# Two small activations of the query factors move one step on in ScalarE's order

## The chip, the cores and the metric

The kernel runs on one core of a Trainium2 chip. The metric is the device time of one launch in microseconds; of several runs the median is told. The engines are called PE (TensorE), DVE (VectorE), ACT (ScalarE), POOL (GpSimd) and SP (SyncE, which issues the transfers here). Each of them takes its own instructions strictly in order and waits for the others on semaphores.

## What is computed

The input is 4 sequences of 512 rows of 128 numbers. A first layer (an attention of 16 heads with alibi) is followed by six local layers, and the change lies in these. One local layer does, cut to what matters:

```
q, k, v = split(shift_tokens(x) @ Wqkv)            # 16 heads of 64
q = l2norm(q) * qs;  k = l2norm(k) * ksc           # then both are rotated by tables
sim  = einsum(q, k of this and the last window of 32) * 8.0,  masked
attn = softmax(sim);  x = (attn @ v) @ Wo + x
xn   = layernorm(shift_tokens(x));  a, gate = split(xn @ W1 + b1)
x    = a * gelu(gate) @ W2 + b2 + x
```

The norm of q is not applied to q. It is kept as one factor for each row and head, `rq = 8 / |q|`, and goes in as the scale of the exponential of the scores: `prob = exp(rq * s_in + lower)`, with `lower = -max(s_in) * rq`.

## The kernel before

The local layers are a software pipeline. A *unit* is one layer of one sequence (24 units), a *quarter* is 4 of the 16 heads of a unit (96 quarters), and a loop over 105 steps `s` is written out on each engine. In step `s` the engines work on several quarters at once: `n = s` is projected and normed, `c = s - 1` is scored, the weights of `d = s - 2` are exponentiated, and those of `e = s - 3` are transposed and applied to the rows (`weigh_rows`). The program's own order on each engine, and nothing else, decides what runs first; `after(engine, semaphore, n)` is a wait for the n-th signal.

The order of ACT in a step is: once in four steps (`s` = 11, 15, ... ) the gelu of a unit, between two loads of the function table (L1010, L1015, L1017); 5, 3 and 8 exponentials of `d` (L1001), with the squares of the k projection between them (`sq`, L1026 and L1031); the squares of the q projection (L1037, L1039); the copies `zT` (L997, two); logarithm and exponential of the key factors `rk` (L1048, L1050); those of the query factors `rq` (L1053, L1055); and once in four steps (`s` = 1, 5, 9, ...) the copy `xk_own` (L997) and the normed rows `xnT` (L1064). Two kinds of step are spoken of below: a **gelu step** is one that begins with the gelu, an **xnT step** is one that ends with `xk_own` and `xnT`.

What stands around these on the other engines:

- PE: k projection (L862), output projection `bank_y` (L881), q projection (L862) into the same `bank_a`, which must wait until both squares of k are taken (`sqk_ok`, L1031), `weigh_rows` (L873), the sum over a key head (L946), scores (L894), the sums over the query heads (L956), turns of the rows (L907, in the xnT step), first half of the feed forward (`bank_f` and `bank_z`, L902: the gate's product is the last thing in the step ahead of a gelu step).
- DVE: the rotation products `pk` and `pq` (L1135 to L1142), the transpose `pT` (L1156), the floor of the key sums (L1178), `den` (L1181), the masked scores `s_in` (L1188, L1190), the floor of the query sums `rq_sum` (L1196, signals `floorq_ok`), the row maxima `s_max` (L1200).
- POOL: `sumk` (L1090), `pk` (L1092, L1093), `sumq` (L1096), `qfin` (L1099, L1100), `kfin` (L1104, L1105, needs `rk`), and at the end of the step `lower` of quarter `c` (L1110, needs `rq` of `c` and `s_max`), for which the exponentials of the next step wait.

Of the kernel before, what the change touches and what calls it, by code (L numbers as in the profile page):

```python
# [14 lines left out]
ACT = mybir.ActivationFunctionType  # L15
# [692 lines left out]
def local_layers(nc, args, state, held):  # L708
# [4 lines left out]
    with ExitStack() as ctx:  # L713
        def sb(name, shape, dt=F32):
            return ctx.enter_context(nc.sbuf_tensor(name, shape, dt))
# [4 lines left out]
        def sem(name):  # L720
# [13 lines left out]
        rq = sb("rq", [P, 2, TPB * GH])  # L734
        rq_sum = sb("rq_sum", [P, TPB * GH])
        log8 = sb("log8", [P, 1])
# [33 lines left out]
        sqk_ok, sqq_ok, lnk_ok, rk_ok, lnq_ok, rq_ok, exp_ok, z01_ok, z23_ok, xk_ok, xnT_ok, gelu_ok = map(  # L770
            sem, ["sqk_ok", "sqq_ok", "lnk_ok", "rk_ok", "lnq_ok", "rq_ok", "exp_ok", "z01_ok", "z23_ok", "xk_ok",
                  "xnT_ok", "gelu_ok"])
        sqk0_ok, sqq0_ok, pk2_ok, pq2_ok = map(sem, ["sqk0_ok", "sqq0_ok", "pk2_ok", "pq2_ok"])
        pk_ok, pq_ok, floor_ok, den_ok, rden_ok, pT_ok, mask_ok, max_ok, floorq_ok, lower_ok = map(
            sem, ["pk_ok", "pq_ok", "floor_ok", "den_ok", "rden_ok", "pT_ok", "mask_ok", "max_ok", "floorq_ok", "lower_ok"])
# [5 lines left out]
        def after(eng, s, n, each=1):  # L781

            if n >= 0:
                eng.wait_ge(s, (n + 1) * each)

        def quarter(n):
            return 0 <= n < QUARTERS

        def unit_at(s, stage):

            u, left = divmod(s - LAG_FF - stage, GROUPS)
            return u if left == 0 and 0 <= u < UNITS else None

        def rows_at(s):

            u, left = divmod(s - 1, GROUPS)
            return u if left == 0 and 0 <= u < UNITS else None

        def layer_of(u):
            return u // B  # L800
# [193 lines left out]
        @block.scalar  # L994
        def _(act):
            def copy(out, in_):
                return act.activation(out, in_, ACT.Copy)  # L997

            def exponentials(n, lo, hi):
                for i in range(lo, hi):  # L1000
                    last = act.activation(prob[:, n % 2, i, :], s_in[:, n % 2, i, :], ACT.Exp,  # L1001
                                          bias=lower[:, n % 2, i:i + 1], scale=rq[:, n % 2, i:i + 1])
                return last

            def step(s):
                n, c, d, e = s, s - 1, s - 2, s - 3
                u_back, u_gelu = unit_at(s, 2), unit_at(s, 4)
                u_rows = rows_at(s)
                if u_gelu is not None:
                    act.preload_act_table(ACT.Gelu)  # L1010
                    after(act, gate_mm, u_gelu)
                    after(act, ff_mm, u_gelu - 1)
                    for j, bank in ((2, bank_f), (0, bank_z[:, 2, :]), (1, bank_z[:, 3, :])):
                        m = min(P, FF - j * P)
                        last = act.activation(hid[0:m, j, :], bank[0:m, :], ACT.Gelu, bias=b_gate[0:m, j:j + 1])  # L1015
                    last.then_inc(gelu_ok, 1)
                    act.preload_act_table_set("natural_log_exp_and_others")  # L1017
                if quarter(d):
                    after(act, lower_ok, d)
                    after(act, pT_ok, d - 2)  # L1020
                    after(act, den_ok, d - 2)
                    exponentials(d, 0, 5)
                if quarter(n):
                    after(act, k_mm, n)
                    after(act, sumq_ok, n - 1)
                    act.activation(sq[:, 0, :], bank_a[:, 0, :], ACT.Square).then_inc(sqk0_ok, 1)  # L1026
                if quarter(d):
                    exponentials(d, 5, 8)
                if quarter(n):
                    after(act, pk2_ok, n)  # L1030
                    act.activation(sq[:, 1, :], bank_a[:, 1, :], ACT.Square).then_inc(sqk_ok, 1)  # L1031
                if quarter(d):
                    exponentials(d, 8, TPB * GH).then_inc(exp_ok, 1)
                if quarter(n):
                    after(act, q_mm, n)
                    after(act, sumk_ok, n)
                    act.activation(sq[:, 0, :], bank_a[:, 0, :], ACT.Square).then_inc(sqq0_ok, 1)  # L1037
                    after(act, pq2_ok, n)
                    act.activation(sq[:, 1, :], bank_a[:, 1, :], ACT.Square).then_inc(sqq_ok, 1)  # L1039
                if quarter(e):  # L1040
                    after(act, z_mm, e)
                    after(act, y_mm, e - 2)
                    z = zT[:, e % 2].rearrange("p w t h q -> p w (t h q)")
                    copy(z[:, 0:2, :], bank_z[:, 0:2, :]).then_inc(z01_ok, 1)
                    copy(z[:, 2:4, :], bank_z[:, 2:4, :]).then_inc(z23_ok, 1)
                if quarter(n):
                    after(act, floor_ok, n)
                    act.activation(rk[:], rk[:], ACT.Ln).then_inc(lnk_ok, 1)  # L1048
                    after(act, lnk_ok, n)
                    act.activation(rk[:], rk[:], ACT.Exp, scale=-0.5).then_inc(rk_ok, 1)  # L1050
                    after(act, floorq_ok, n)
                    after(act, lower_ok, n - 2)
                    act.activation(rq[:, n % 2], rq_sum[:], ACT.Ln).then_inc(lnq_ok, 1)  # L1053
                    after(act, lnq_ok, n)
                    act.activation(rq[:, n % 2], rq[:, n % 2], ACT.Exp, bias=log8[:], scale=-0.5).then_inc(rq_ok, 1)  # L1055
                if u_rows is not None:
                    after(act, xk_mm, u_rows)
                    after(act, z_mm, 4 * (u_rows - 2) + 3)
                    copy(xk_own[:, u_rows % 2].rearrange("p t c -> p (t c)"), bank_z[:, 2, :]).then_inc(xk_ok, 1)
                if u_back is not None:  # L1060
                    after(act, ffn_loaded, layer_of(u_back), 16)
                    after(act, xnT_mm, u_back)
                    after(act, lin_mm, u_back - 1)
                    act.activation(xnT[:], bank_z[:, 3, :], ACT.Identity, bias=ln_b, scale=ln_g).then_inc(xnT_ok, 1)  # L1064

            act.preload_act_table_set("natural_log_exp_and_others")
            act.wait_ge(const_ok, 1)
            for s in range(STEPS_ALL):
                step(s)
# [418 lines left out]
```

## Time and profile before

| what | value |
|---|---|
| median of 3 runs | 2041.87 us (2039.39 to 2042.81) |
| the profiled execution, its time | 2042.99 us |
| its span, first to last instruction | 2040.9 us |
| mean granted TensorE clock | 0.968 |
| busy: PE, DVE, ACT, POOL | 90%, 76%, 68%, 62% |

The local layers take the span from about 420 us to 2016 us. From about 580 us on they repeat with one period for each unit (four steps), and a busy share is a mean over steps of different kinds, so the timeline of one period tells more than the shares do.

### The profile page before, as it was taken

The numbers are of one execution on the slowest core, as the hardware profiler recorded it, in microseconds if no ns is written. First come the engines' busy times: TensorE is split into PE (matmuls) and PEld (weight loads), VectorE is DVE, ScalarE is ACT, GpSimd is POOL, SyncE is SP. The second block draws the span as 40 slices with busy tenths as digits, with TensorE's granted clock in tenths as the row PEclk, the third lists the DMA queues.
The fourth block names the chain that finished last, engine by engine and source line by source line (L and its number), as shares of the span: only waits on it lengthen the run. The fifth ranks groups of instructions, "written<-read, shape, count | busy, mean of one in ns | idle before, by whom it ended". The sixth has DMA issues, their size and how long they took to land. (4 is left out here: it accounts for less than half of the span.)

```text
span 2040.9 us, 47434 instructions
## 1 busy us (share of the span) xinstructions
PE 1835.3 (90%) x18048; PEld 1023.9 (50%) x18048; DVE 1544.4 (76%) x2543; ACT 1383.9 (68%) x2862; POOL 1263.2 (62%) x1127
## 2 busy tenths in 40 slices
PE   5898898668999999999999999999999999999984
PEld 3443344524555555555555555555555555555541
DVE  4778886257877788788887888878887788877753
ACT  1454445237777777877778777778777877778851
POOL 4303300057877777777777787777877778777721
PEclk8899999769999999999999999999999999999996
DMA  9000000215323343233432234332343322233300
GB/s 192 2 2 1 2 2 2 63 46 98 75 69 75 81 89 75 68 71 82 87 80 69 68 81 86 74 79 68 75 88 74 83 68 69 67 77 84 71 22 21
DMA packets 142992, 131.86 MB, mean 65 GB/s; under 512 B 85160, under 2 KB 88808, under 8 KB 142440
## 3 DMA queue, kind: packets, MB, share of 16 engines
q1 hardware_dynamic: 142768, 128.83, 28.4%
q8 instruction: 145, 2.38, 0.5%
q14 instruction: 79, 0.65, 0.1%
HBM read 20.94 MB, written 1.05 MB: 11 GB/s over the span
## 5 line engine op out<-in xcount | busy, mean ns | idle before, releaser
L1001 ACT ACTIVATE prob<-s_in,lower,rq 128x64 f32<-128x64 f32 x1536 | 537.9, 430 | 79.0 <-POOL lower L1110 77.0
L862 PE MATMUL bank_a<-x_shift,wqk_sb 128*128 128x512 f32 x768 | 375.2, 612 | 69.1 <-ACT sq L1031 57.5
L881 PE MATMUL bank_y<-zT,wvo 128*128 128x512 f32 x768 | 345.2, 592 | 0.0
L1090 POOL TENSOR_TENSOR sumk<-sq 128x512 f32<-128x512 f32 x96 | 122.3, 1274 | 271.6 <-ACT sq L1031 271.6
L862 PEld LDWEIGHTS bank_a<-x_shift,wqk_sb 128*128 128x128 f32 x768 | 140.1, 193 | 262.0 <-issue 148.4
L881 PEld LDWEIGHTS bank_y<-zT,wvo 128*128 128x128 f32 x768 | 146.0, 190 | 183.7 <-issue 183.7
L894 PEld LDWEIGHTS bank_z<-kpad,qpair 128*32 128x32 f32 x6144 | 164.6, 110 | 100.1 <-issue 98.8
L894 PE MATMUL bank_z<-kpad,qpair 128*32 128x128 f32 x6144 | 187.7, 274 | 23.2 <-ACT zT L997 23.2
L491 DVE TENSOR_REDUCE a_negmax<-a_max 128x1 f32<-128x512 f32 x256 | 164.7, 685 | 47.9 <-PE a_max L166 44.3
L382 ACT ACTIVATE a_prob<-a_sT 128x1024 f32<-128x1024 f32 x128 | 130.5, 1023 | 103.7 <-PE a_sT L216 101.8
L997 ACT ACTIVATE zT<-bank_z 128x1024 f32<-128x1024 f32 x192 | 186.1, 1023 | 10.7 <-PE bank_z L873 8.0
L1078 POOL TENSOR_TENSOR prob<-prob,rden 128x1024 f32<-128x1024 f32 x96 | 182.9, 1905 | 3.9 <-DVE rden L1184 3.9
L1096 POOL TENSOR_TENSOR sumq<-sq 128x512 f32<-128x512 f32 x96 | 122.0, 1270 | 92.5 <-ACT sq L1039 92.5
L873 PE MATMUL bank_z<-pT,xk_prev 32*128 32x128 f32 x3072 | 164.8, 284 | 3.2 <-DVE xn L1162 1.7
L873 PEld LDWEIGHTS bank_z<-pT,xk_prev 32*128 32x128 f32 x3072 | 122.4, 187 | 78.4 <-issue 56.1
L873 PE MATMUL bank_z<-pT,xk_own 32*128 32x128 f32 x3072 | 154.8, 271 | 0.0
L1135 DVE SCALAR_TENSOR_TENSOR pk<-bank_a,scale_sb,rot_sb 128x512 f32<-128x512 f32 x96 | 71.8, 748 | 104.3 <-PE bank_a L862 94.3
L461 POOL TENSOR_TENSOR a_rstd<-a_mv,eps 128x4 f32<-128x4 f32 x4 | 0.8, 198 | 232.8 <-DVE a_mv L549 232.8
L1099 POOL TENSOR_TENSOR qfin<-pq 128x512 f32<-128x512 f32 x96 | 123.7, 1289 | 0.0
L873 PEld LDWEIGHTS bank_z<-pT,xk_own 32*128 32x128 f32 x3072 | 123.0, 188 | 0.0
L1141 DVE SCALAR_TENSOR_TENSOR pk<-bank_a,scale_sb,rot_sb 128x512 f32<-128x512 f32 x96 | 71.6, 746 | 67.6 <-ACT sq L1026 67.6
L1104 POOL TENSOR_TENSOR kfin<-rk,pk 128x512 f32<-128x512 f32 x96 | 122.1, 1272 | 0.5 <-ACT rk L1050 0.5
(161 smaller groups left out, 3947.3 us busy)
## 6 DMA issues: line engine op xcount, KB each, us to landing
qpair<-qfin SPq DMA_DIRECT2D x384, 128.0 KB, 2.3
kpad<-kfin SPq DMA_DIRECT2D x768, 64.0 KB, 2.0
wqk_sb<-in_wqkv SPq DMA_DIRECT2D x24, 256.0 KB, 5.6
xk_prev<-xk_own SPq DMA_DIRECT2D x24, 192.0 KB, 2.4
ffn_sb<-in_ffn SPq DMA_DIRECT2D x6, 537.5 KB, 3.9
wv_in<-in_wqkv SPq DMA_DIRECT2D x12, 256.0 KB, 4.8
wo_in<-in_wo SPq DMA_DIRECT2D x6, 512.0 KB, 5.8
xk_prev<-xk_own SPq DMA_DIRECT2D x24, 48.0 KB, 2.1
```

Of the source, the lines that this page charges most:

```text
L382: act.activation(prob[:, j % 2, 2 * half:2 * half + 2, :], sT_bank[:, 2 * half:2 * half + 2, :], ACT.Exp).then_inc(exp_ok, 1)
L491: dve.tensor_reduce(negmax[:, unit // 4, unit % 4:unit % 4 + 1], max_bank[u % 2][:], AX.X, ALU.max, negate=True).then_inc(max_ok, 1)
L862: last = pe.matmul(bank_a[:, half, :], wqk_sb[:, layer_of(u) % 2, part, half, g * P:(g + 1) * P], cols(u), start=True, stop=True)
L873: last = pe.matmul(bank_z[:, w, t * P:(t + 1) * P], rows[at, u % 2, t, :], pT[at, n % 2, c, t * GH:(t + 1) * GH, :].rearrange("p h q -> p ...
L881: last = pe.matmul(bank_y[:].rearrange("p (t w q) -> p t w q", w=WPT, q=WIN), wvo[:, layer_of(u), GH * g + hh, :], zT[:, n % 2, :, :, hh, ...
L894: last = pe.matmul(bank_z[WIN * w:WIN * w + WIN, t // 2, c:c + P], qpair[:, p, at:at + WIN], kpad[:, p, :, at:at + 2 * WIN], start=True, s ...
L997: return act.activation(out, in_, ACT.Copy)
L1001: last = act.activation(prob[:, n % 2, i, :], s_in[:, n % 2, i, :], ACT.Exp, bias=lower[:, n % 2, i:i + 1], scale=rq[:, n % 2, i:i + 1])
L1078: pool.tensor_tensor(prob[:, e % 2], prob[:, e % 2], rden[:].unsqueeze(2).broadcast_to([P, TPB * GH, 2 * WIN]), ALU.mult).then_inc(pn_ok, 1)
L1090: pool.tensor_tensor(sumk[:], sq[:, 0, :], sq[:, 1, :], ALU.add).then_inc(sumk_ok, 1)
L1099: pool.tensor_tensor(qfin[:, 0, :], pq[:, 0, :], pq[:, 1, :], ALU.subtract)
L1104: pool.tensor_tensor(kfin[:, 0, :], rk[:], pk[:, 0, :], ALU.mult)
```

## The change

The two activations of `rq` leave the end of step `n`, and stand in step `n + 1` (where that quarter is `c`), behind the gelu and its second table load and ahead of the exponentials of `d`. Their two waits move with them. Nothing is added, removed or resized on any engine.

```diff
@@ act step(s) @@
                     last.then_inc(gelu_ok, 1)
                     act.preload_act_table_set("natural_log_exp_and_others")
+                if quarter(c):
+                    after(act, floorq_ok, c)
+                    after(act, lower_ok, c - 2)
+                    act.activation(rq[:, c % 2], rq_sum[:], ACT.Ln).then_inc(lnq_ok, 1)
+                    after(act, lnq_ok, c)
+                    act.activation(rq[:, c % 2], rq[:, c % 2], ACT.Exp, bias=log8[:], scale=-0.5).then_inc(rq_ok, 1)
                 if quarter(d):
                     after(act, lower_ok, d)
                     after(act, pT_ok, d - 2)
...
                     after(act, lnk_ok, n)
                     act.activation(rk[:], rk[:], ACT.Exp, scale=-0.5).then_inc(rk_ok, 1)
-                    after(act, floorq_ok, n)
-                    after(act, lower_ok, n - 2)
-                    act.activation(rq[:, n % 2], rq_sum[:], ACT.Ln).then_inc(lnq_ok, 1)
-                    after(act, lnq_ok, n)
-                    act.activation(rq[:, n % 2], rq[:, n % 2], ACT.Exp, bias=log8[:], scale=-0.5).then_inc(rq_ok, 1)
```

In a step that ends without `xk_own` and is followed by one without gelu nothing stood between the two places, so ACT's order is the same there. It differs at two places.

The first is ACT at the border from step 10 to step 11, the first gelu step. Before, the pair of `rq` stands ahead of the table load:

```order
L1048 ACTIVATE rk<-rk 128x512
L1050 ACTIVATE rk<-rk 128x512
L1053 ACTIVATE rq<-rq_sum 128x16
L1055 ACTIVATE rq<-rq,log 128x16
L1010 ACT_TABLE_LOAD
L1015 ACTIVATE hid<-bank_f,ffn_sb 85x512
L1015 ACTIVATE hid<-bank_z,ffn_sb 128x512 x2
L1017 ACT_TABLE_LOAD
L1001 ACTIVATE prob<-s_in,lower,rq 128x64 x5
```

Now it stands between the second load and the exponentials (the lines of the changed file are six further on behind the added lines):

```order
L1054 ACTIVATE rk<-rk 128x512
L1056 ACTIVATE rk<-rk 128x512
L1010 ACT_TABLE_LOAD
L1015 ACTIVATE hid<-bank_f,ffn_sb 85x512
L1015 ACTIVATE hid<-bank_z,ffn_sb 128x512 x2
L1017 ACT_TABLE_LOAD
L1021 ACTIVATE rq<-rq_sum 128x16
L1023 ACTIVATE rq<-rq,log 128x16
L1001 ACTIVATE prob<-s_in,lower,rq 128x64 x5
```

The pair moved past two table loads and three gelus.

The second is ACT at the border from step 9 to step 10, the end of an xnT step. Before:

```order
L1050 ACTIVATE rk<-rk 128x512
L1053 ACTIVATE rq<-rq_sum 128x16
L1055 ACTIVATE rq<-rq,log 128x16
L997 ACTIVATE xk_own<-bank_z 128x512
L1064 ACTIVATE xnT<-bank_z,ffn_sb 128x512
L1001 ACTIVATE prob<-s_in,lower,rq 128x64 x5
```

And now:

```order
L1056 ACTIVATE rk<-rk 128x512
L997 ACTIVATE xk_own<-bank_z 128x512
L1065 ACTIVATE xnT<-bank_z,ffn_sb 128x512
L1021 ACTIVATE rq<-rq_sum 128x16
L1023 ACTIVATE rq<-rq,log 128x16
L1001 ACTIVATE prob<-s_in,lower,rq 128x64 x5
```

Here it moved past one copy and one activation. PE, DVE, POOL and SP keep their instructions and their order.

## Rows read from the trace of the kernel before

**Rows 1.** The page: busy time by engine, and the slices.
```profile
PE 1835.3 (90%) x18048; PEld 1023.9 (50%) x18048; DVE 1544.4 (76%) x2543; ACT 1383.9 (68%) x2862; POOL 1263.2 (62%) x1127
...
PE   5898898668999999999999999999999999999984
...
PEclk8899999769999999999999999999999999999996
```

**Rows 2.** Windows, from one unit's first gelu to the next one's.
```profile
580.18:644.44 64.26, 61.35 (x647) 35.23 (x646) 52.22 (x83) 50.20 (x111) 49.09 (x43) 1.00 0.31 71
1030.00:1094.24 64.24, 61.34 (x647) 35.23 (x646) 52.23 (x83) 50.19 (x111) 49.06 (x43) 1.00 0.33 80
1865.38:1929.63 64.25, 61.35 (x647) 35.23 (x646) 52.22 (x83) 50.21 (x111) 49.05 (x43) 1.00 0.30 71
```

**Rows 3.** Waits between 580 and 1945 us: total, times, longest.
```profile
POOL sumk L1090 <- ACT sq L1031: 244.6, 85, 5.4
...
ACT rq L1053 <- DVE rq_sum L1196: 123.2, 84, 1.5
...
ACT prob L1001 <- POOL lower L1110: 59.3, 42, 1.5
...
PE bank_a L862 <- ACT sq L1031: 41.1, 22, 1.9
```

**Rows 4.** Timeline of ACT around one gelu step.
```profile
1025.66 0.63 ACT L1050 ACTIVATE rk<-rk 128x512 f32<-128x512 f32 x1
1027.75 0.22 ACT L1053 ACTIVATE rq<-rq_sum 128x16 f32<-128x16 f32 x1 [1.47 <-DVE rq_sum L1196]
1028.00 0.31 ACT L1055 ACTIVATE rq<-rq,log 128x16 f32<-128x16 f32 x1
1028.33 1.28 ACT L1010 ACT_TABLE_LOAD   x1
1030.00 0.68 ACT L1015 ACTIVATE hid<-bank_f,ffn_sb 85x512 f32<-85x512 f32 x1 [0.39 <-PE bank_f L902]
1030.58 1.25 ACT L1015 ACTIVATE hid<-bank_z,ffn_sb 128x512 f32<-128x512 f32 x2
1031.85 1.28 ACT L1017 ACT_TABLE_LOAD   x1
1033.14 1.76 ACT L1001 ACTIVATE prob<-s_in,lower,rq 128x64 f32<-128x64 f32 x5
...
1036.28 0.58 ACT L1031 ACTIVATE sq<-bank_a 128x512 f32<-128x512 f32 x1
```

**Rows 5.** Timeline of PE in the same stretch.
```profile
1027.14 1.96 PE L902 MATMUL bank_z<-xnT,ffn_sb 128*128 128x512 f32 x4
1028.94 1.02 PE L902 MATMUL bank_f<-xnT,ffn_sb 128*85 128x512 f32 x2
1029.80 1.88 PE L862 MATMUL bank_a<-x_shift,wqk_sb 128*128 128x512 f32 x4
1031.51 3.60 PE L881 MATMUL bank_y<-zT,wvo 128*128 128x512 f32 x8
1036.98 1.95 PE L862 MATMUL bank_a<-x_shift,wqk_sb 128*128 128x512 f32 x4 [1.87 <-ACT sq L1031]
```

**Rows 6.** DVE and POOL in the same stretch.
```profile
1035.42 0.75 DVE L1141 SCALAR_TENSOR_TENSOR pk<-bank_a,scale_sb,rot_sb 128x512 f32<-128x512 f32 x1 [2.30 <-ACT sq L1026]
...
1036.93 1.28 POOL L1090 TENSOR_TENSOR sumk<-sq 128x512 f32<-128x512 f32 x1 [5.44 <-ACT sq L1031]
```

**Rows 7.** Timeline of all engines at the end of one xnT step.
```profile
1013.78 0.31 ACT L1055 ACTIVATE rq<-rq,log 128x16 f32<-128x16 f32 x1
...
1013.99 0.58 ACT L997 ACTIVATE xk_own<-bank_z 128x512 f32<-128x512 f32 x1
...
1014.47 0.77 ACT L1064 ACTIVATE xnT<-bank_z,ffn_sb 128x512 f32<-128x512 f32 x1
...
1015.05 0.23 POOL L1110 TENSOR_TENSOR lower<-s_max,rq 128x16 f32<-128x16 f32 x1
...
1015.32 1.10 ACT L1001 ACTIVATE prob<-s_in,lower,rq 128x64 f32<-128x64 f32 x3
```

**Rows 8.** PE there, its q projection in the next step too.
```profile
1012.91 0.64 PE L907 MATMUL bank_z<-ident,x_shift 128*128 128x128 f32 x4
1013.39 0.60 PE L907 MATMUL bank_z<-ident,xn 128*128 128x128 f32 x4
...
1019.15 1.96 PE L862 MATMUL bank_a<-x_shift,wqk_sb 128*128 128x512 f32 x4
```

## The prediction

> **What bounds the kernel now.** I read the page first, then the waits, then one period engine by engine. The page says that PE is busy for 90% of the span and ACT for 68%, with the clock near full in the local layers [rows 1]. That alone would say that ACT has room and that two activations of 16 columns may stand anywhere. The windows from gelu to gelu show how regular the pipeline is: each unit takes 64.25 us, at a granted clock of 1.00 (the higher level, 2.4 GHz), and PE is busy for 61.35 us of it [rows 2]. So PE is idle for 2.90 us in a period, and the question is only where these are and who makes them. The waits between 580 and 1945 us answer it: PE waits for `sq` L1031 22 times, 41.1 us in all, which is 1.87 us each [rows 3]. There are 22 gelu steps in which exponentials follow (steps 11, 15, ... 95), so this is one stall in each gelu step, and PE idles for hardly more than a microsecond elsewhere in the period (2.90 - 1.87 = 1.03 us).
>
> The reader is to see the gelu step in the timelines. ACT loads the gelu's table at 1028.33, has it at 1029.61, waits 0.39 us for the gate's product, starts the gelus at 1030.00, loads the other table at 1031.85 and starts the exponentials at 1033.14 with no gap; the square of k that frees `bank_a` starts at 1036.28 and ends at 1036.86 [rows 4]. PE is through with `bank_y` at 1035.11, and its q projection starts at 1036.98, 0.12 us after the square's end, with the 1.87 us of idleness ahead of it [rows 5]. DVE waits in the same step for the square ahead of it (2.30 us), and POOL for L1031 (5.44 us) [rows 6]. So in a gelu step all three other engines wait for ACT, and ACT itself runs without a gap from 1030.00 to that square. ACT, which is idle for a third of the time, is the bound of this stretch.
>
> **The change part by part.** Nothing is removed or added; one pair moves, with its semaphores. No transfer is issued by it, and no queue but ACT's is touched.
>
> *Where the order stays.* In two of four steps the pair keeps its place between `rk` and the exponentials: no cost and no gain. The wait for `rq_sum` (1.47 us) and the one for `lower` that follows it go on as they are there.
>
> *Gelu step, what it gains.* The pair today waits 1.47 us for DVE's `rq_sum`, and ends at 1028.31. Without it ACT can load the gelu's table as soon as `rk` is done, at 1026.29, that is 2.04 us earlier [rows 4]. That is worth nothing: the gelus wait for the gate's product, whose last matmul ends at 1028.94 + 1.02 = 1029.96 [rows 5], and the gelu starts 0.04 us later. That matmul stands behind four others that run without a gap, so PE's own order sets it. The table load then ends at about 1027.58, and ACT waits 2.43 us in place of 0.39.
>
> *Gelu step, what it costs.* The pair now stands behind the second table load, in the stretch where ACT has no gap. From the start of the logarithm to that of the exponential are 0.25 us, and from there to the next activation 0.21 us where the next one waits for nothing (1013.78 to 1013.99) [rows 4, 7]; its inputs are long there, since `rq_sum` is done before 1027.75. So the exponentials start at 1033.14 + 0.46 = 1033.60 (`lower` came at about 1029.6 and isn't waited for). The bounds: without any overlap it is 0.22 + 0.03 + 0.31 = 0.56 us; below 0.46 I see nothing, since the second activation needs the first one's result. Before, these 0.46 us were covered by ACT's wait for the gate; that cover is gone.
>
> The Trainium skill, page ScalarE: Activation LUTs, section What ACT_TABLE_LOAD costs, says that an ACTIVATE with immediates takes 186 ns + 0.833 ns a column, that a pointer operand adds about 93 ns, and that neighbours overlap by about 93 ns. By it the two take 199 and 292 ns, as the rows have them, and if both overlapped the pair would cost about 0.31 us, which by 22 would be some 7 us, a median of about 2048.7. The row is against the first overlap: 0.25 us from start to start, since the exponential waits for the logarithm.
>
> *Who is late next.* `sq` L1026 and L1031 come 0.46 us later, since the 5 and 3 exponentials stand ahead of them. PE's q projection follows L1031 by 0.12 us, so its stall grows from 1.87 to 2.33 us. DVE's products and POOL's `sumk` also wait for these squares and shift by as much. No engine passes the gelu step unshifted, so nothing downstream can give the time back, and the period becomes 64.25 + 0.46 = 64.71 us.
>
> *xnT step.* Here the pair moves behind `xk_own` and `xnT`. Before: `rq` ends at 1014.09, `xk_own` starts at 1013.99, `xnT` ends at 1015.24, and the exponentials start at 1015.32, just behind `lower` (1015.05 + 0.23 = 1015.28) [rows 7]. Now `xk_own` has to wait for PE's turn, which ends at 1013.55 [rows 8]; it starts at about 1013.59, `xnT` 0.48 us later at 1014.07, the logarithm after another 0.67 us (0.77 less the overlap of 0.1) at 1014.74, its exponential at 1014.99, and ACT is free for the weights at 1015.20. `lower` lets them go at 1015.32, as before. So this costs nothing, but with only 0.12 us to spare. What lies behind that has no cover: the PE's q projection of the next step starts at 1019.15 and the square ends at about 1019.04, the same 0.11 us apart as in the stalled step [rows 8].
>
> *The sum.* 22 gelu steps by 0.46 us are 10.1 us. The profiled execution took 2042.99 us (span 2040.9 and 2.1 around it), and would take 2053.1. The median of the runs shown is 1.12 us below it, so the predicted median is 2041.87 + 10.1 = 2052.0 us, 0.5% slower. About 0.2% (4 us) is what a measurement of this kernel tells from no change.
>
> **The rivals.**
>
> *The xnT step loses too.* If nothing overlaps there, the exponentials start at 1013.59 + 0.58 + 0.77 + 0.56 = 1015.50, and if the turn's signal comes 0.1 us later than its modelled end, at 1015.60, 0.28 us late. With 0.56 us in the gelu step, that is 22 x (0.56 + 0.28) = 18.5 us, 2060.4. For it speaks that the spare time is small and the ends of matmuls are modelled; against it that neighbours overlap by 0.1 us in all rows of ACT. 0.09.
>
> *No change.* The 0.46 us would have to be absorbed: the PE's stall would have to be a shadow of something else, for instance of the DVE or POOL, which then come no later. Then the time is 2041.9. Against it is that both also wait for ACT in that step [rows 6]; nothing in the profile speaks for it but that the square's end and PE's start are inferred. 0.05.
>
> *Faster.* The mechanism would be the earlier table load. If the gate's product were ready by the time the load ends, at about 1027.6, the exponentials would start 2.43 us earlier and 0.46 later, 1.97 us in net, and PE's stall of 1.87 would vanish: 22 x 1.87 = 41 us, 2001 us. It decides from the point at which the gate's product is ready 0.46 us sooner than 1029.96. Against it is the wait of 0.39 us that ACT already has there, in each of the 22 steps with the same length, and that PE has no gap in front of the product [rows 4, 5]. It would need PE to reach the gate earlier, for instance because `xk_own` and `xnT` are ready 0.4 us sooner, and no row shows PE waiting for them. 0.04.
>
> **How the numbers follow.** The forecast has a chance of 0.82, and its own range is 2041.87 + 22 x 0.46 to 22 x 0.56, 2052 to 2054, widened by the scatter of the medians (2.5 us down to 2039.39, 0.9 up), 2049.5 to 2055. The range on record goes a little below and well towards the first rival, 2048.5 to 2057; outside are the two small rivals (0.09) and most of the first. Slower by over 0.2% is 0.82 + 0.09 = 0.91, of which I give up 0.02 for what I haven't seen; within 0.2% 0.06, faster 0.05.
>
> **What the changed profile would show.** The windows from gelu to gelu are 64.7 us. ACT's wait for `bank_f` ahead of the gelu is 2.4 us. The exponentials follow `rq` by some 0.2 us in the gelu step, 3.6 us after the gelu's start in place of 3.14. PE's stall there is 2.3 us, 22 times. ACT's waits for `rq_sum` go from 84 to about 40 in the same stretch. The exponentials behind an xnT step still start at `lower`, with a wait of about 0.1 us. The forecast is wrong if the period stays at 64.25, which would mean an absorbed delay, or if it grows by over 0.6 us, which would mean that the xnT step has lost too.

## The result and the profile after

The changed kernel takes 2055.8 us (median of 4 runs, 2053.65 to 2057.62), the kernel before 2042.07 (4 runs, 2039.39 to 2042.81). The ratio is 1.0068, with a 95% interval of 1.0052 to 1.0084: slower by 13.7 us. The forecast was 2052.0, in a range of 2048.5 to 2057.

These are the windows of the changed kernel from gelu to gelu, with the columns of [rows 2] (span; busy time of PE, weight loads, DVE, ACT and POOL; granted clock; share of the DMA engines; GB/s):

```profile
578.86:644.97 66.11, 62.99 (x647) 35.60 (x646) 52.21 (x83) 50.32 (x111) 49.03 (x43) 0.97 0.30 69
644.97:709.67 64.70, 61.34 (x647) 35.23 (x646) 52.21 (x83) 50.09 (x111) 49.07 (x43) 1.00 0.30 70
968.48:1034.50 66.02, 62.91 (x647) 35.72 (x646) 52.22 (x83) 50.30 (x111) 49.02 (x43) 0.97 0.44 85
1681.81:1747.86 66.05, 62.94 (x647) 35.71 (x646) 52.21 (x83) 50.30 (x112) 49.05 (x43) 0.97 0.30 69
```

There are two kinds of period now. The plain one has 64.70 us, which is 0.45 above the 64.25 of [rows 2] and 0.01 below the forecast. Between the first and the last of the 22 gelu steps lie 21 periods, and three of them have 66.0 to 66.1 us: some 1.35 us more, at a mean granted clock of 0.97 in place of 1.00. Before, none of the 21 was more than 0.16 us above the shortest.

The timeline of ACT in a gelu step after (against [rows 4]), around the start of one of these long periods:

```profile
964.79 1.28 ACT L1010 ACT_TABLE_LOAD   x1
968.48 0.68 ACT L1015 ACTIVATE hid<-bank_f,ffn_sb 85x512 f32<-85x512 f32 x1 [2.41 <-PE bank_f L902]
969.06 1.25 ACT L1015 ACTIVATE hid<-bank_z,ffn_sb 128x512 f32<-128x512 f32 x2
970.33 1.28 ACT L1017 ACT_TABLE_LOAD   x1
971.62 0.22 ACT L1021 ACTIVATE rq<-rq_sum 128x16 f32<-128x16 f32 x1
971.87 0.31 ACT L1023 ACTIVATE rq<-rq,log 128x16 f32<-128x16 f32 x1
972.08 1.75 ACT L1001 ACTIVATE prob<-s_in,lower,rq 128x64 f32<-128x64 f32 x5
...
975.21 0.58 ACT L1037 ACTIVATE sq<-bank_a 128x512 f32<-128x512 f32 x1
```

The exponentials start 3.60 us after the gelu (3.14 before), the wait ahead of the gelu has grown from 0.39 to 2.41 us, and the pair takes 0.46 us from its start to the first exponential. The first table load now starts 3.69 us ahead of the gelu in place of 1.67, and the 2.02 us between the two have only made ACT's wait for the gate's product longer.

The timeline of PE in the same step, and below it in an ordinary one (against [rows 5]):

```profile
969.99 3.60 PE L881 MATMUL bank_y<-zT,wvo 128*128 128x512 f32 x8
975.90 3.52 PE L862 MATMUL bank_a<-x_shift,wqk_sb 128*128 128x512 f32 x4 [2.31 <-ACT sq L1037]
...
1036.02 3.60 PE L881 MATMUL bank_y<-zT,wvo 128*128 128x512 f32 x8
1041.93 1.96 PE L862 MATMUL bank_a<-x_shift,wqk_sb 128*128 128x512 f32 x4 [2.31 <-ACT sq L1037]
```

The stall is 2.31 us in both (1.87 before). But the same q projection takes 3.52 us at 975.90, and 1.96 us at 1041.93. The windows around 975.90, with the same columns, tell why:

```profile
973.00:974.50 1.50, 0.59 (x2) 0.00 (x0) 0.15 (x1) 1.50 (x5) 0.00 (x0) 1.00 0.39 93
974.50:976.00 1.50, 0.10 (x1) 0.13 (x1) 1.50 (x3) 1.50 (x5) 0.14 (x1) 0.88 1.19 187
976.00:977.00 1.00, 1.00 (x2) 0.48 (x3) 1.00 (x2) 1.00 (x4) 1.00 (x1) 0.50 1.38 159
977.00:978.00 1.00, 1.00 (x3) 0.48 (x2) 0.99 (x2) 1.00 (x4) 1.00 (x2) 0.50 1.57 148
978.00:979.00 1.00, 1.00 (x2) 0.08 (x1) 0.18 (x1) 0.43 (x2) 1.00 (x2) 0.50 1.64 146
979.00:980.00 1.00, 1.00 (x21) 0.65 (x24) 0.54 (x1) 0.54 (x1) 0.58 (x1) 0.97 1.63 156
```

The granted clock falls to 0.50, the lower level of 1.2 GHz, toward the end of PE's 2.31 us of idleness, and is back at 1.00 some 3.4 us later; for about 3 us of these PE works at the lower level. Below, such a stretch is called a **fall** of the clock. In the two other long periods the fall starts at the same place to within half a microsecond, once just behind the start of the q projection (at 586.5 us, the gap ending at 586.3). The Trainium skill (TensorE: Matmul & The Clock Gate, Part 1: The HAM clock gate) says that activity releases the throttle and idleness brings it back, and that there are two levels; the trace agrees, with 1.00 and 0.50.

The xnT step (against [rows 7, 8]), the rows of ACT and POOL out of the timeline of all engines:

```profile
1018.09 0.60 ACT L997 ACTIVATE xk_own<-bank_z 128x512 f32<-128x512 f32 x1 [1.52 <-PE bank_z L907]
...
1018.59 0.77 ACT L1065 ACTIVATE xnT<-bank_z,ffn_sb 128x512 f32<-128x512 f32 x1
1019.26 0.20 ACT L1021 ACTIVATE rq<-rq_sum 128x16 f32<-128x16 f32 x1
1019.50 0.31 ACT L1023 ACTIVATE rq<-rq,log 128x16 f32<-128x16 f32 x1
1019.57 0.22 POOL L1111 TENSOR_TENSOR lower<-s_max,rq 128x16 f32<-128x16 f32 x1
...
1019.82 1.76 ACT L1001 ACTIVATE prob<-s_in,lower,rq 128x64 f32<-128x64 f32 x5
```

`lower` ends at 1019.79 and the exponentials start 0.03 us later; ACT was free at 1019.71 (0.21 us after the start of L1023). So this step has lost nothing, with about 0.1 us to spare.

### The profile page after: what moved, and what is told of

Read it like the earlier page. It is cut to its first block and busy times, and to the rows that moved or that the text cites. A ratio compares the mean times of both kernels' runs of the same rounds, so it can differ in the third digit from the quotient of the medians.

```text
span 2055.8 us, 47434 instructions
## 1 busy us (share of the span) xinstructions
PE 1842.2 (90%) x18048; PEld 1024.3 (50%) x18048; DVE 1543.4 (75%) x2543; ACT 1382.3 (67%) x2862; POOL 1263.0 (61%) x1127
## 5 line engine op out<-in xcount | busy, mean ns | idle before, releaser
L862 PE MATMUL bank_a<-x_shift,wqk_sb 128*128 128x512 f32 x768 | 380.1, 619 | 79.0 <-ACT sq L1037 67.6
L1100 POOL TENSOR_TENSOR qfin<-pq 128x512 f32<-128x512 f32 x96 | 123.7, 1288 | 0.0
L1101 POOL TENSOR_TENSOR qfin<-pq 128x512 f32<-128x512 f32 x96 | 122.3, 1274 | 0.0
```

The costliest lines, as they stand in the source:

```text
L862: last = pe.matmul(bank_a[:, half, :], wqk_sb[:, layer_of(u) % 2, part, half, g * P:(g + 1) * P], cols(u), start=True, stop=True)
L1100: pool.tensor_tensor(qfin[:, 0, :], pq[:, 0, :], pq[:, 1, :], ALU.subtract)
L1101: pool.tensor_tensor(qfin[:, 1, :], pq[:, 2, :], pq[:, 3, :], ALU.add).then_inc(qfin_ok, 1)
```

## The experiments

Theory after the result: a plain gelu step costs 0.45 us (22 of them, 9.9 us), and the rest of the 13.7 us, some 4 us, are three falls of TensorE's clock at the longer stall. The rivals: the rest comes from the xnT step, or from a wait that has nothing to do with the clock.

**The gelu step alone.** The pair moves only where a gelu step follows (`query_factors` is the pair with its two waits):

```diff
                     act.preload_act_table_set("natural_log_exp_and_others")
+                    if quarter(c):
+                        query_factors(c)
...
-                    after(act, floorq_ok, n)
...
+                    if unit_at(s + 1, 4) is None:
+                        query_factors(n)
```

> The pair of rq moves behind the gelu only where a gelu step follows; at the end of an xnT step it stays ahead of xk_own and xnT, as before. Theory (the gelu step pays for all of it, and PE's longer stall lets its clock fall now and then): the same as the whole change, about 2055.8 us, period 64.70, stall 2.31 us. Rival (the part of the 13.7 us that the forecast of 10.1 lacks, some 4 us, comes from the xnT step): about 2052 us.

Measured: 2057.18 us (2054.69 to 2057.88), against 2041.64 for the kernel before on the same chip, ratio 1.0073 (1.0061 to 1.0086). The plain periods have 64.70 us, and again three of the 21 have 66.1. The whole of the loss is in the gelu step.

**The xnT step alone.** The pair stays in its step, but behind `xnT`:

```diff
-                    after(act, floorq_ok, n)
...
                     act.activation(xnT[:], bank_z[:, 3, :], ACT.Identity, bias=ln_b, scale=ln_g).then_inc(xnT_ok, 1)
+                if quarter(n):
+                    after(act, floorq_ok, n)
...
```

> The pair of rq moves behind xk_own and xnT, but stays in its own step, ahead of the gelu. Theory: no change, 2042 us, exponentials behind an xnT step still start at lower. Rival (the xnT step costs what the forecast lacks): about 2046 us.

Measured: 2042.77 us (11 runs), ratio 1.0004 (0.9995 to 1.0013), and the first period as a window:

```profile
578.07:642.33 64.26, 61.35 (x647) 35.22 (x646) 52.20 (x83) 50.23 (x112) 49.12 (x43) 1.00 0.31 71
```

There is no change, and none of its 21 periods is a long one. This rules out the xnT step as the source of what is lacking, and with it the first rival of the prediction.

**The stall filled.** To the changed kernel two products that nobody reads are added, which PE computes in its stall; nothing else is altered:

```diff
                     project_out(h)
+                u_gelu = unit_at(s, 4)
+                if u_gelu is not None and quarter(n):
+                    after(pe, gelu_ok, u_gelu)
+                    after(pe, floorq_ok, c)
+                    for _ in range(2):
+                        pe.matmul(bank_f[:], ident[:], xnT[:], start=True, stop=True)
```

> The whole change, and PE computes two products that nobody reads, into bank_f, in each gelu step between the output projection and the q projection, 1.7 us of its stall of 2.31. Theory (three to four falls of TensorE's clock after the longer stall, 1.35 us each, are what the forecast lacks): no such falls, period 64.70 throughout, about 2052 us. Rival (what is lacking has another cause): 2056 us, the outlying periods stay.

Measured: 2054.17 us (2049.94 to 2057.24), ratio 1.0059 (1.0046 to 1.0071). PE in a gelu step:

```profile
649.79 1.88 PE L881 MATMUL bank_y<-zT,wvo 128*128 128x512 f32 x4
651.51 1.88 PE L932 MATMUL bank_f<-xnT,ident 128*128 128x512 f32 x4
653.99 1.96 PE L862 MATMUL bank_a<-x_shift,wqk_sb 128*128 128x512 f32 x4 [0.60 <-ACT sq L1043]
```

The q projection still waits for ACT's square and starts as late as without the filling, but only 0.60 us of the gap is idle. All 21 periods have 64.69 to 64.87 us, at a clock of 1.00. The falls are gone: 21 periods take 1359.09 us (581.85 to 1940.94), where the gelu-only kernel took 1363.05 (579.04 to 1942.09) and the whole change 1363.10. That is 4.0 us, three falls of 1.3. The median is 3.0 us under the gelu-only one, in the right direction, but the two spreads of 5 runs overlap, so by the median alone this experiment would not settle it: the first gelu alone lies anywhere between 577 and 582 us in these profiles.

**Twice the cost.** A second pair behind the second load, on spare data:

```diff
                     act.preload_act_table_set("natural_log_exp_and_others")
+                    if quarter(c):
+                        after(act, spare_ok, 2 * u_gelu - 1)
+                        act.activation(spare[:, 0], ident[:, 0:16], ACT.Exp).then_inc(spare_ok, 1)
+                        after(act, spare_ok, 2 * u_gelu)
+                        act.activation(spare[:, 1], spare[:, 0], ACT.Exp, bias=log8[:], scale=-0.5).then_inc(spare_ok, 1)
```

> The whole change, and behind the gelu's second table load a second pair of 16-column activations on spare data. Theory: each gelu step 0.46 us longer still, period about 65.16, stall 2.77 us, and with the longer stall more falls of the clock than the 3 of 22: 2055.8 + 10 + some 2 to 8 for the falls, 2068 to 2074 us. Rival without the clock: exactly as much again as the change has cost in a plain period, 0.44 x 22, 2065.5 us.

Measured: 2086.76 us (2086.47 to 2088.49), ratio 1.0222 (1.0208 to 1.0236), well over what either theory said. The windows:

```profile
580.37:646.90 66.53, 62.93 (x647) 36.34 (x646) 52.20 (x83) 50.69 (x113) 49.22 (x43) 0.97 0.28 68
...
713.35:778.52 65.17, 61.34 (x647) 35.22 (x646) 52.21 (x83) 50.53 (x113) 49.15 (x43) 1.00 0.44 86
```

The plain period is 65.17, as expected, but only 4 of 21 are plain; the other 17 have 66.35 to 66.6 us, at a clock of 0.97. PE's stall is 2.76 us in all of them:

```profile
588.24 2.43 PE L864 MATMUL bank_a<-x_shift,wqk_sb 128*128 128x512 f32 x4 [2.76 <-ACT sq L1044]
654.77 3.48 PE L864 MATMUL bank_a<-x_shift,wqk_sb 128*128 128x512 f32 x4 [2.76 <-ACT sq L1044]
```

In some of these periods the clock falls ahead of the gap's end, in others over a microsecond behind it, inside the q projection, which is why the first row has 2.43 us and the second 3.48. I had the mechanism and had the number of falls far too low.

**Twice the cost, filled.** This is the same kernel with the two unread products of the filled stall.

> The doubled pair of the run before, and PE computes two unread products into bank_f in each gelu step ahead of its q projection. Theory (the steps of 66.5 us in the doubled kernel are plain steps of 65.17 and a fall of TensorE's clock): no falls, period 65.17 throughout, some 29 us less than 2086.8, about 2064 us. Rival (the second pair costs so much by itself, through a wait): about 2087 us.

Measured: 2063.12 us (2059.87 to 2067.66), ratio 1.0104 (1.0089 to 1.0118), 23.6 us less than without the filling, by adding work to the busiest engine. The first period:

```profile
578.26:643.41 65.15, 63.06 (x651) 35.99 (x650) 52.22 (x83) 50.52 (x113) 49.12 (x43) 1.00 0.29 70
```

All 21 are 65.14 to 65.29, at a clock of 1.00, and PE's idle gap ahead of the q projection is 1.04 us. So the second pair by itself costs 0.45 us a step, and what the doubled kernel's periods had above that went with the falls. Two pairs come to 22 x 0.90 = 19.8 us in the periods; the median is 21.7 us above the kernel before, and the 1.9 us between the two are within the spread of these runs.

**The second pair ahead of the gelu.** This is the changed kernel with the spare pair in front of the gelu's table load:

```diff
                 if u_gelu is not None:
+                    if quarter(c):
+                        after(act, spare_ok, 2 * u_gelu - 1)
...
                     act.preload_act_table(ACT.Gelu)
```

> The whole change, and the second pair on spare data stands ahead of the gelu's table load instead of behind the second one. Theory (ACT has 2.41 us of cover there, since the gelu waits for the gate's product): no cost, about 2056 us, period 64.70, the wait ahead of the gelu 0.5 us shorter at about 1.9. Rival (the earlier arrival at the gelu is worth something, or ACT's own work there counts): 0.46 x 22 more, about 2066 us.

Measured: 2055.85 us (2051.26 to 2060.04), ratio 1.0068 (1.0054 to 1.0083), the same ratio as the changed kernel's. ACT there:

```profile
637.94 0.20 ACT L1014 ACTIVATE spare<-ident 128x16 f32<-128x16 f32 x1
638.18 0.31 ACT L1016 ACTIVATE spare<-spare,log 128x16 f32<-128x16 f32 x1
638.50 1.28 ACT L1017 ACT_TABLE_LOAD   x1
641.75 0.68 ACT L1022 ACTIVATE hid<-bank_f,ffn_sb 85x512 f32<-85x512 f32 x1 [1.96 <-PE bank_f L904]
```

The wait ahead of the gelu is 1.96 us in place of 2.41, and the plain period is 64.71; two of the 21 have a fall. The same two instructions are free ahead of the gelu and cost 0.45 us behind it.

**Squares first.** If three engines wait for ACT's squares in a gelu step, these should not stand behind 8 exponentials. From the kernel before, in gelu steps alone:

```diff
                     last.then_inc(gelu_ok, 1)
+                    if quarter(n):
+                        first_square(n)
                     act.preload_act_table_set("natural_log_exp_and_others")
+                    if quarter(n):
+                        second_square(n)
...
-                if quarter(n):
+                if quarter(n) and u_gelu is None:
...
```

> The kernel before, but in a gelu step ACT takes the first square of k between the gelus and the second table load and the second square right behind it, and the 16 exponentials then run in one piece. Theory (PE, DVE and POOL wait in a gelu step for these squares): PE's stall of 1.87 us there goes; ACT is then the bound up to zT, and keeps all its work but the 0.75 us that it waits for DVE's products, so the period is some 0.6 us shorter: 22 x 0.6, about 2028 us. Rival (the stall only moves to where PE waits for zT): 2042 us.

Measured: 2025.04 us (2021.69 to 2025.59), ratio 0.9913 (0.9901 to 0.9925): 16.4 us faster than the kernel before on the same chip, and 30.8 below the changed kernel's 2055.8 (measured apart from it). ACT in a gelu step, and PE's two waits around it:

```profile
706.78 0.59 ACT L1008 ACTIVATE sq<-bank_a 128x512 f32<-128x512 f32 x1
707.38 1.28 ACT L1028 ACT_TABLE_LOAD   x1
708.68 0.60 ACT L1012 ACTIVATE sq<-bank_a 128x512 f32<-128x512 f32 x1
709.17 5.39 ACT L1001 ACTIVATE prob<-s_in,lower,rq 128x64 f32<-128x64 f32 x16
714.47 0.58 ACT L1047 ACTIVATE sq<-bank_a 128x512 f32<-128x512 f32 x1
714.95 0.58 ACT L1049 ACTIVATE sq<-bank_a 128x512 f32<-128x512 f32 x1
715.42 1.92 ACT L997 ACTIVATE zT<-bank_z 128x1024 f32<-128x1024 f32 x2
```

```profile
706.57 3.60 PE L881 MATMUL bank_y<-zT,wvo 128*128 128x512 f32 x8
710.00 1.88 PE L862 MATMUL bank_a<-x_shift,wqk_sb 128*128 128x512 f32 x4
...
716.58 1.69 PE L894 MATMUL bank_z<-kpad,qpair 128*32 128x128 f32 x53 [1.65 <-ACT zT L997]
```

The stall ahead of the q projection is gone, and one of 1.65 us stands ahead of the scores in place of 0.41: ACT has no gap left from the gelu to `zT`. This is how the squares of q and the scores stood in the kernel before:

```profile
718.10 0.59 ACT L1037 ACTIVATE sq<-bank_a 128x512 f32<-128x512 f32 x1
719.43 0.60 ACT L1039 ACTIVATE sq<-bank_a 128x512 f32<-128x512 f32 x1 [0.74 <-DVE pq L1136]
...
721.09 1.96 PE L894 MATMUL bank_z<-kpad,qpair 128*32 128x128 f32 x64 [0.41 <-ACT zT L997]
```

The period is 63.39 us, 0.86 shorter; I had said 0.6, from DVE's 0.75 us alone. The two squares of q now start 0.48 us apart in place of 1.33, which is 0.85 of it. So the rival is half right (the stall moves to `zT`), and the gain is what ACT itself no longer waits for. The periods give 22 x 0.86 = 18.9 us, the medians 16.4: the profiled execution was the fastest of the five, and none shows where the others lost the difference.

**Squares first, with the pair behind the gelu.** The changed kernel, with the squares moved in the same way and the pair behind them.

> The changed kernel with the squares ahead of the second load and right behind it, and the pair of rq behind them. Theory: PE's stall goes with its falls of the clock, but ACT is the bound of the step up to zT, so the pair still costs its 0.46 us in each gelu step against the same kernel without it: about 2038 us, 10 above the run with the pair ahead of the gelu. Rival (the pair cost only by the squares that it held up): the same time as that run.

Measured: 2059.75 us (2056.15 to 2064.18), ratio 1.0088 (1.0074 to 1.0103). The shortest windows are 63.84, 0.45 above the run before, as the theory has it. But 11 of 21 are longer. One of each, and the clock in the gelu step of the long one:

```profile
576.96:640.80 63.84, 61.10 (x647) 35.30 (x646) 52.12 (x83) 50.01 (x111) 49.13 (x43) 1.00 0.31 71
640.80:706.21 65.41, 62.67 (x647) 36.80 (x646) 52.13 (x83) 50.02 (x112) 49.16 (x43) 0.97 0.30 69
```

```profile
650.00:652.50 2.50, 0.69 (x2) 0.00 (x0) 1.21 (x2) 2.50 (x6) 0.68 (x1) 1.00 0.00 0
652.50:654.00 1.50, 1.21 (x24) 1.24 (x28) 1.50 (x3) 1.50 (x3) 1.50 (x2) 0.54 0.00 0
```

The row of the scores in that step:

```profile
652.79 3.50 PE L894 MATMUL bank_z<-kpad,qpair 128*32 128x128 f32 x62 [2.10 <-ACT zT L997]
```

PE's idle gap ahead of the scores is 2.10 us here, and the clock falls at its end. The column of the DMA engines has 0.00 in the two windows above, and over 1 in those of the changed kernel's fall, so the traffic isn't what the falls have in common. "PE's stall goes with its falls of the clock" was wrong: the stall had moved, and where it stands now it draws more falls than the 2.31 us ahead of the q projection do. The expected 2038 us missed by 22. The pair costs 34.7 us in this kernel against the one without it, of which 22 x 0.45 = 9.9 are its own time; the eleven long periods of the profiled execution hold 26.3 us above the plain 63.84. That these are the clock's is read from the trace: no filled version of this kernel was run.

## Why the prediction was right, and where it was short

- *What bounds the kernel.* Right. The gelu step alone holds the loss (2057.18 against 2042.77 for the xnT step alone), and putting the squares ahead of the exponentials there gains 16.4 us.
- *What the gelu step gains: nothing.* Right. The wait was forecast at 2.43 us and is 2.41, and a second pair in that cover was free.
- *What it costs: 0.46 us.* Right: from the pair's start to the exponentials 0.46 us, and 0.45 us in the period. The overlap of about 93 ns that the Trainium skill has (ScalarE: Activation LUTs, What ACT_TABLE_LOAD costs), which for both would have made it 0.31, isn't there between the two, since the second waits for the first: 0.25 us from start to start. The rows have 0.22 and 0.31 us for them, 0.02 above the 199 and 292 ns that the prediction worked out.
- *Who is late next.* Right in the place and in the first order: the stall was forecast at 2.33 us and is 2.31, the period at 64.71 and is 64.70.
- *xnT step.* Right: no loss, 0.1 us to spare.
- *The sum.* Here a term is missing. "22 gelu steps by 0.46 us are 10.1 us" measured 9.9. It took a longer stall of PE to cost its own length. It costs more: in 3 of the 21 periods of the profiled execution the clock falls to the lower level around the end of the stall, the q projection behind it takes 3.5 us in place of 1.96, and the period is some 1.35 us longer. That is 4 us, and with the 9.9 it comes to 13.9 beside the 13.7 of the medians; how many falls the other executions had isn't known. The profiles' own difference of 14.9 us has besides 1.3 us less ahead of the first gelu and 2.2 us more between the last two (23.39 us in place of 21.16). The latter doesn't follow the change: the xnT-only kernel has 23.34 there, and the two doubled ones, which hold the whole change, have 21.39 and 21.33. The clock is at the lower level for part of that stretch in every kernel, the one before included.
- *The range.* That 2055.8 lies in it is in part luck. The forecast's own range was 2049.5 to 2055, and missed; the upper end of 2057 was set toward the first rival, a loss in the xnT step, which did not come about. The prediction's own sign of being wrong would have misled too: the mean period grew by 0.65 us, over the 0.6 that "would mean that the xnT step has lost too", and the xnT step had lost nothing.
- *The rivals.* None of them came about. The clock was none of them, though [rows 2] had it at 1.00 in spite of a stall of 1.87 us: I read that row as "the clock is full" and did not ask what a longer stall would do to it.

What stays open: why the clock falls in 3 periods and not in the other 18, which look alike in all rows (one of these even has a gap of 2.48 us, without a fall), and how the count of falls follows from a gap's length and place.

## What to carry to other kernels

An instruction is free or dear by the wait that stands behind it on its engine, not by its length or by the engine's busy share: look for the last stretch before the others' wait in which the engine has no gap, and move work out of it. What others wait for goes to the front of such a stretch. When a change makes PE idle longer at a stretch, price the clock beside the length, and test it by filling the gap with products that nobody reads: if what follows starts no earlier and the time falls all the same, it was the clock.

## What the runs showed of the hardware

I had not expected that the clock would answer so steeply. Ahead of the q projection: 1.87 us of idleness, no fall in 21 periods; 2.31 us, 3 falls (3 in the gelu-only kernel too, 2 in the one with the spare pair ahead of the gelu); 2.76 us, 17 falls. Filled down to 0.60 and 1.04 us, none. Ahead of the scores: 1.65 us, none; 2.10 us, 11. A fall cost 1.2 to 1.7 us in most periods, 3.3 in one of the last kernel and 5.0 in two (68.84 in place of 63.85). The clock stayed at the lower level for some 3.4 us in most falls, for some 7 us where a fall cost 3.3, and for some 10 us where it cost 5.0 (from 1430.9 and from 1758.5 us on), with PE busy all the while. Adding 1.7 us of matmuls in each of 22 steps made a kernel 23.6 us faster.
